# Transposes of six of sixteen FFN blocks move from the matrix engine to 96 SBUF transfers and 12 VectorE transposes

## The chip, the cores and the metric

The kernel runs on one core of a Trainium2 chip. The metric is the device time of one execution in microseconds (us), the lower the better. The engines are named as the profile names them: PE (TensorE, the matrix engine; PEld is its weight loads), DVE (VectorE), ACT (ScalarE), POOL (GpSimd) and SP (SyncE, which here only issues transfers).

## The reference

The input is 4096 rows (two sequences of 2048) of 256 numbers, all float32. A feed-forward part, a linear attention and the feed-forward part again are each added to the rows; each works on rows that were normalized first.

```python
x = x + 0.5 * ffn(layernorm(x), W_r, W_k, W_v, mu_r, mu_k)
x = x + attention(layernorm(x), Wq, Wk, Wv, Wu, Wo)
x = x + 0.5 * ffn(layernorm(x), W_r, W_k, W_v, mu_r, mu_k)
# ffn:
x_prev = concatenate([zeros, x[:, :-1, :]])          # the row before, 0 ahead of a sequence
xr = mu_r * x + (1 - mu_r) * x_prev
xk = mu_k * x + (1 - mu_k) * x_prev
out = sigmoid(xr @ W_r) * (square(relu(xk @ W_k)) @ W_v)
# attention, 16 heads of 16:
q, k = relu(x @ Wq) / 4, relu(x @ Wk) / 4            # v = x @ Wv, u = silu(x @ Wu)
out = (srms_norm(q @ (k.T @ v)) * u) @ Wo
```

## The kernel before

The rows are cut into 8 blocks of 512 (four tiles of 128 rows). "FFN n" is the feed-forward part on block n for n = 0 to 7 (the first one) and on block n - 8 for n = 8 to 15 (the second one). Each product in float32 is made of three in float32r, from operands split in a rounded part (`_hi`) and a rest (`_lo`), so most of the work of ACT, DVE and POOL is splitting.

For the mixing of FFN n the normalized rows `xn` must stand with the features on the partitions, since `mu` goes by features and the row before is then the column before. Before the change eight 128x128 transposes on PE do that (`transpose_a(n)`, L1296), from `xn` into the PSUM tile `psA`. From `psA` ACT takes the previous-row part (`previous`, L635), DVE adds the current-row part (`mix_current`, L948), ACT and POOL split the mix in `mix_k_hi` (`mix_high`, L668) and `mix_k_lo` (`k_low`, L427), and ACT and DVE the other one in `mix_r_hi` and `mix_r_lo` (`r_low`, L976). `xn` is one buffer, and its scales come from `stats_a` (DVE, L917), `scales_a` (POOL, L402 to L411) and `normalize` (ACT, L618).

Each engine has its instructions written out by hand in one order, and a wait on a semaphore holds all that stands behind it on that engine. The part of the program that matters here is a loop over i = 1 to 6 on ACT, DVE and POOL ("iteration i") with the same on PE. In iteration i, PE does `ffn_k(i)` (into `psK`), `transpose_a(i + 1)`, `transpose_b(i - 1)` (rows of the attention, L1410), `ffn_r(i)`, `k_and_u(i - 1)` (keys and gates of the attention), `ffn_v(i)`, `gram(i - 1)` (into `psK`, reads `k_hi` and `k_lo`) and `q_of(i - 1)`. All products show as lines L1279 to L1281. Iterations 5 and 6 and the part behind them hold attention outputs too (`attend`, `transpose_g`, `project_out`; `gate_heads` and `head_norms` on DVE). Behind iteration 6, FFN 7 is done without a next mix, and FFN 8 is mixed apart.

Four waits tie the engines together at the places below. `k_and_u` waits for `x2_low` of DVE (L1024), which waits for `x2_high` of ACT (L712). `gram` waits for both halves of `k_lo` (`kt_low` on POOL, L479), which waits for `kt_high` of ACT (L722). `ffn_k(i + 1)` waits for `keep_g(i - 1)` of DVE (L1048 for a batch's first block, L1051), since both use the first bank of `psK`. And `normalize` waits for the last of the four instructions of `scales_a`. SP only issues: 17 loads at the start, and the stores of the last stage, each behind its wait.

Of the kernel before, what the change touches and what calls it, by code (L numbers as in the profile page):

```python
# [45 lines left out]
def macaron(nc, x, w_t, mu_r, mu_k, out):  # L46
# [6 lines left out]
    with ExitStack() as ctx:  # L53
# [3 lines left out]
        def sem(name):  # L57
            return ctx.enter_context(nc.semaphore(name))
# [233 lines left out]
        def prev_part(n, rk, h):  # L292

            return mix_part(n, rk, h) + n

        def half(g):
            return slice(g * D, (g + 1) * D)

# [47 lines left out]
        def _(sp):  # L346
# [22 lines left out]
            sp.dma_start(wo[:], weight_rows("o")).then_inc(s_w_in["o"], 16)  # L369
            for b in range(3, NB):  # L370
                load_x(b)
            for b in range(NB - 1):
                store_x(b)
            for t in range(TILES):
# [7 lines left out]
        def _(pool):  # L382
# [150 lines left out]
            for i in range(1, 6):  # L533
                act_low(i)
                k_low(i + 1)
                if i > 1:
                    kt_low(i - 1)
                scales_a(i + 2)
                scales_b(i)
                x1_low(i)  # L540
                if i == 1:
                    weight_sum("v")
                if i == 2:
                    pool.wait_ge(s_wo_hi, 1)
                    nc.gpsimd.tensor_tensor(wo_lo[:], wo[:], wo_hi[:].bitcast(F32), ALU.subtract).then_inc(s_wo_lo, 1)
# [48 lines left out]
        def _(act):  # L594
# [202 lines left out]
            for i in range(1, 7):  # L797
                front(i, i + 1, i - 1)
                sigmoid_u(i - 1, 0)
                sigmoid_r(i, 1)  # L800
                sigmoid_u(i - 1, 1)
                if i > 1:
                    kt_high(i - 1, 0)
                sigmoid_u(i - 1, 2)
                sigmoid_u(i - 1, 3)
                if i > 1:
                    kt_high(i - 1, 1)
                if i == 6:
                    keep_g_rows(0)
                mix_high(i + 1, 1)  # L810
                if i <= 5:
                    normalize(i + 2)
                if i >= 5:
                    square_heads(i - 5)
                x1_high(i)
                if i == 2:
                    act.wait_ge(s_w_in["o"], 16)
                    nc.scalar.activation(wo_hi[:], wo[:], ACT.Identity).then_inc(s_wo_hi, 1)
                relu_q(i - 1)
# [70 lines left out]
        def _(dve):  # L890
# [53 lines left out]
            def mix_one(n, rk, h):  # L944

                dve.wait_ge(s_prev, prev_part(n, 1, h))
                m = mix[:, rk, h, :]
                nc.vector.scalar_tensor_tensor(out=m, in0=psA[:, h, :], scalar=mu[:, rk, h:h + 1], in1=m,  # L948
                                               op0=ALU.mult, op1=ALU.add).then_inc(s_mix, 1)

            def mix_first(rk, g, h):

# [226 lines left out]
            for i in range(1, 7):  # L1179
                if 1 < i <= 5:  # L1180
                    stats_a(i + 2)
                x2_low(i - 1)
                mix_current(i + 1)
                if i == 1:
# [29 lines left out]
            add_attention(1)  # L1214
            stats_b(7)
            gate_heads(2)
            head_norms(2)
            x2_low(7)
            keep_g(6)
# [57 lines left out]
        def _(pe):  # L1277
# [283 lines left out]
            q_of(0, (s_silu, 2))  # L1561
            for i in range(2, 5):
                ffn_k(i, [(s_gacc, i - 1)])
                transpose_a(i + 1, [(s_wcen, 4)] if i == 4 else [])
                transpose_b(i - 1)
                ffn_r(i)
                k_and_u(i - 1)
# [5 lines left out]
            kv(0, [(s_halo, 7)])  # L1573

            ffn_k(5, [(s_gacc, 4)])
            transpose_a(6, [(s_kvbd, 1)])
            transpose_b(4)
            ffn_r(5)
            k_and_u(4)
# [3 lines left out]
            q_of(4, (s_silu, 18))  # L1583

            ffn_k(6, [(s_gacc, 5)])
            transpose_a(7, [(s_gu, 2)])
            transpose_b(5)
            ffn_r(6)
            k_and_u(5)
# [14 lines left out]
            attend(2, [(s_gu, 4)])  # L1604
            q_of(6, (s_x2, 4))

            transpose_a(8, [(s_gu, 6)])
            transpose_b(7)
            gram(6)
            k_and_u(7)  # L1610
# [64 lines left out]
```

## Time and profile before

| | |
|---|---|
| time, median of 3 runs | 312.41 us (312.12 to 312.45) |
| the profiled execution | 312.87 us, span of the core 311.1 us |
| PE busy | 303.8 us, 98% of the span |
| DVE / ACT / POOL busy | 240.4 / 235.6 / 214.8 us (77 / 76 / 69%) |
| granted clock of PE | 1.00 from 46 us to the end |
| transfers | 10.85 MB, of which hardly any between 37 us and 230 us |

The profiled execution took 312.87 us, of which 1.8 us lie outside the core's span. Busy shares tell which engine is full, but each matrix product ends later than the next one starts, so for PE the starts of its weight loads are the better clock: a group of eight or of twelve ends where the next group's first weight load starts.

### The profile page before, as it was taken

The page shows a single profiled execution, that of the slowest core. Times are in us where ns is not written, and L with a number is a line of the kernel's source. Part 1 is how long each engine was busy: PE and PEld are TensorE (multiplying, and loading weights), DVE is VectorE, ACT ScalarE, POOL GpSimd, SP SyncE. Part 2 cuts the span into 40 slices and gives each one's busy share as a digit, 9 for nine tenths or more (in the row PEclk, how much of TensorE's full clock was granted, in tenths as well). Part 3 has the DMA queues.
Part 4 walks back from the last instruction along what each step waited for, and adds up shares of the span by engine and source line. Part 5 has one row for each costly group of instructions (what it writes and reads, how often), then busy time and mean ns, then how long its engine had stood idle before and what let it go on. Part 6 is the DMA issues. An engine that isn't in the chain of part 4 may idle for free.

```text
span 311.1 us, 5822 instructions
## 1 busy us (share of the span) xinstructions
PE 303.8 (98%) x2044; PEld 276.8 (89%) x2044; DVE 240.4 (77%) x586; ACT 235.6 (76%) x461; POOL 214.8 (69%) x236
## 2 busy tenths in 40 slices
PE   6899999999999999999999999999999999999995
PEld 6688889889988988988988998989999999999984
DVE  2989893585666746896894699586979797999695
ACT  2886958879589579679349548669797979699981
POOL 4387978779777688669269314815798979769833
PEclk9999999999999999999999999999999999999999
DMA  7960000000000000000000000000001010101023
GB/s 207 382 223 0 1 3 0 0 2 0 2 1 3 0 0 2 0 2 0 0 3 1 2 0 0 2 1 3 0 3 67 2 67 16 54 2 67 32 106 135
DMA packets 10752, 10.85 MB, mean 35 GB/s; under 512 B 482, under 2 KB 10724, under 8 KB 10724
## 3 DMA queue, kind: packets, MB, share of 16 engines
q1 hardware_dynamic: 10432, 10.23, 9.6%
q8 instruction: 16, 0.26, 0.4%
q10 hardware_dynamic: 292, 0.26, 0.2%
q14 instruction: 12, 0.10, 0.1%
HBM read 6.29 MB, written 4.19 MB: 34 GB/s over the span
## 4 chain that ended last, share of the span: by engine, by line
PE 79%; DVE 12%; ACT 4%; issue 2%; POOL 1%; DVEq 0%; ACTq 0%; POOLq 0%
PE psK L1279 7%; PE psK L1281 7%; PE psK L1280 7%; PE psX L1279 7%; PE psX L1281 7%; PE psX L1280 7%; PE psRV L1280 6%; PE psRV L1279 6%; PE psRV L1281 6%; PE psA L1296 3%; DVE mix L948 3%; PE psA L1483 2%; PE psX L1410 2%; PE psX L1496 2%; PE psK L1483 2%
## 5 line engine op out<-in xcount | busy, mean ns | idle before, releaser
L948 DVE SCALAR_TENSOR_TENSOR mix<-psA,mu,mix 128x512 f32<-128x512 f32 x60 | 41.5, 744 | 11.4 <-ACT mix L635 11.4
L618 ACT ACTIVATE xn<-xs,shiftA,rstdA 128x256 f32<-128x256 f32 x53 | 27.7, 607 | 15.9 <-POOL shiftA L411 15.9
L427 POOL TENSOR_TENSOR mix_k_lo<-mix,mix_k_hi 128x512 fp32r<-128x512 f32 x26 | 33.3, 1301 | 8.5 <-ACT mix_k_hi L668 8.5
L635 ACT ACTIVATE mix<-psA,one_mu 128x511 f32<-128x511 f32 x60 | 36.9, 697 | 0.6 <-PE psA L1296 0.6
L1279 PE MATMUL psRV<-ffn_hi,mix_r_hi 128*128 128x256 f32 x120 | 34.3, 286 | 0.0
L1281 PE MATMUL psRV<-ffn_hi,mix_r_lo 128*128 128x256 f32 x120 | 33.6, 280 | 0.0
L1280 PE MATMUL psRV<-ffn_lo,mix_r_hi 128*128 128x256 f32 x120 | 33.5, 280 | 0.0
L1279 PE MATMUL psRV<-ffn_hi,act_hi 128*128 128x256 f32 x96 | 27.5, 286 | 0.0
L1280 PE MATMUL psRV<-ffn_lo,act_hi 128*128 128x256 f32 x96 | 26.8, 279 | 0.0
L1281 PE MATMUL psRV<-ffn_hi,act_lo 128*128 128x256 f32 x96 | 26.8, 279 | 0.0
L479 POOL TENSOR_TENSOR k_lo<-k_tok,k_hi 128x512 fp32r<-128x512 f32 x14 | 18.1, 1295 | 11.4 <-ACT k_hi L722 11.4
L917 DVE BATCH_NORM_STATS2 statsA<-xs 128x6 f32<-128x256 f32 x64 | 22.4, 413 | 2.6 <-DMA xs<-x_dram 2.5
L1279 PE MATMUL psK<-mix_k_hi,ffn_hi 128*128 128x512 f32 x60 | 24.1, 402 | 0.0
L470 POOL TENSOR_TENSOR x_lo<-xs,x_hi 128x512 fp32r<-128x512 f32 x14 | 17.8, 1295 | 8.6 <-ACT x_hi L717 8.6
L1281 PE MATMUL psK<-mix_k_hi,ffn_lo 128*128 128x512 f32 x60 | 23.5, 392 | 0.0
L1280 PE MATMUL psK<-mix_k_lo,ffn_hi 128*128 128x512 f32 x60 | 23.4, 391 | 0.0
L1279 PEld LDWEIGHTS psRV<-ffn_hi,mix_r_hi 128*128 128x128 f32 x120 | 22.5, 188 | 0.4 <-issue 0.2
L1280 PEld LDWEIGHTS psRV<-ffn_lo,mix_r_hi 128*128 128x128 f32 x120 | 22.6, 188 | 0.2
L1281 PEld LDWEIGHTS psRV<-ffn_hi,mix_r_lo 128*128 128x128 f32 x120 | 22.5, 187 | 0.0
L1024 DVE TENSOR_TENSOR x_lo<-psX,x_hi 128x512 fp32r<-128x512 f32 x16 | 10.3, 683 | 14.4 <-ACT x_hi L712 14.4
L668 ACT ACTIVATE mix_k_hi<-mix 128x512 fp32r<-128x512 f32 x30 | 18.8, 658 | 1.9 <-DVE mix L948 1.8
L668 ACT ACTIVATE mix_r_hi<-mix 128x512 fp32r<-128x512 f32 x30 | 17.7, 648 | 0.8 <-DVE mix L948 0.8
(204 smaller groups left out, 1084.5 us busy)
## 6 DMA issues: line engine op xcount, KB each, us to landing
xs<-x_dram SPq DMA_DIRECT2D x7, 512.0 KB, 7.8
out_dram<-xs SPq DMA_DIRECT2D x7, 512.0 KB, 2.9
out_dram<-xs SPq DMA_DIRECT2D x4, 128.0 KB, 1.8
xs<-x_dram ACTq DMA_DIRECT2D x2, 128.0 KB, 3.0
xs<-x_dram SPq DMA_DIRECT2D x2, 128.0 KB, 2.8
silu_u<-w_ffn_k_dram SPq DMA_DIRECT2D x1, 256.0 KB, 5.1
silu_u<-w_ffn_r_dram SPq DMA_DIRECT2D x1, 256.0 KB, 6.2
q_store<-w_k_dram SPq DMA_DIRECT2D x1, 256.0 KB, 6.4
```

The costliest lines, as they stand in the source:

```text
L427: nc.gpsimd.tensor_tensor(mix_k_lo[:, h, :], mix[:, 0, h, :], mix_k_hi[:, h, :].bitcast(F32), ALU.subtract).then_inc(s_lo_k, 1)
L470: nc.gpsimd.tensor_tensor(x1_lo[:, g * BANK:(g + 1) * BANK], row(xs, a, g * BANK, BANK), x1_hi[:, g * BANK:(g + 1) * BANK].bitcast(F32), A ...
L479: nc.gpsimd.tensor_tensor(k_lo[:, tiles, :], k_tok[:, tiles, :], k_hi[:, tiles, :].bitcast(F32), ALU.subtract).then_inc(s_kt_lo, 1)
L618: nc.scalar.activation(xn[:, t, :], tile_row(xs, b, t), ACT.Identity, bias=shiftA[:, t:t + 1], scale=rstdA[:, t:t + 1]).then_inc(s_xn, 1)
L635: nc.scalar.activation(mix[:, rk, h, 1:BLOCK], psA[:, h, 0:BLOCK - 1], ACT.Copy, scale=one_mu[:, rk, h:h + 1]).then_inc(s_prev, 1)
L668: nc.scalar.activation(hi[:, h, :], mix[:, rk, h, :], ACT.Identity).then_inc(done, 1)
L917: nc.vector.bn_stats(statsA[:, t, :], tile_row(xs, b, t)).then_inc(s_bnA, 1)
L948: nc.vector.scalar_tensor_tensor(out=m, in0=psA[:, h, :], scalar=mu[:, rk, h:h + 1], in1=m, op0=ALU.mult, op1=ALU.add).then_inc(s_mix, 1)
L1279: nc.tensor.matmul(dst, a_hi, b_hi, start=start, stop=False)
L1280: nc.tensor.matmul(dst, a_hi, b_lo, start=False, stop=False)
L1281: return nc.tensor.matmul(dst, a_lo, b_hi, start=False, stop=stop)
L1483: last = nc.tensor.matmul(ps[:, t // 2, (t % 2) * D + h * P:(t % 2) * D + (h + 1) * P], q_half(j, h)[:, tok(t)], kv_bd[:, j // BB, h, :], ...
```

## The change

For FFN 3 to 8 (`TURNED`) PE no longer transposes. Instead SP waits until all four tiles of `xn` are written and issues 16 transfers of 32 partitions x 8 x 32 numbers (32 KB each) inside SBUF. They put block column j of `xn` on partition group j of a spare buffer (`squares` for FFN 3 to 5, `wsum` for FFN 6 to 8), in pieces of 32 numbers (128 bytes). DVE waits for all 16 (`s_quads`) and turns the 32x32 blocks with two instructions (`turn`), one for each half of the features, straight into `psA`. Beside that, ACT's `normalize(i + 2)` now stands ahead of `mix_high(i + 1, 1)`, and POOL's `scales_a(i + 2)` ahead of `kt_low(i - 1)`. The spare buffers are not new.

```diff
@@ sync
+            for n in TURNED:
+                sp.wait_ge(*normalized(n, TILES - 1))
+                for j in range(QUADS):
+                    for i in range(QUADS):
+                        rows = quads_of(n)[j * QUAD:(j + 1) * QUAD, i * D:(i + 1) * D]
+                        sp.dma_start(rows.rearrange("c (th f) -> c th f", f=QUAD),
+                                     xn[i * QUAD:(i + 1) * QUAD, :, :].rearrange(
+                                         "c t (h j f) -> c (t h) j f", h=HALVES, j=QUADS)[:, :, j, :]
+                                     ).then_inc(s_quads, 16)
             for b in range(NB - 1):
                 store_x(b)
@@ gpsimd
                 k_low(i + 1)
+                scales_a(i + 2)
                 if i > 1:
                     kt_low(i - 1)
-                scales_a(i + 2)
                 scales_b(i)
@@ scalar
-                mix_high(i + 1, 1)
                 if i <= 5:
                     normalize(i + 2)
+                mix_high(i + 1, 1)
@@ vector
+            def turn(n, free=()):
+                for s, v in free:
+                    dve.wait_ge(s, v)
+                dve.wait_ge(s_halo, n + 1)
+                dve.wait_ge(s_quads, 16 * QUADS * QUADS * (n - TURNED[0] + 1))
+                rows = quads_of(n).rearrange("p (i t h f) -> p h t i f", i=QUADS, t=TILES, h=HALVES)
+                for h in range(HALVES):
+                    nc.vector.transpose(psA[:, h, :].rearrange("p (t i c) -> p t i c", t=TILES, i=QUADS),
+                                        rows[:, h, :, :, :]).then_inc(s_tA, 1)
...
                     stats_a(i + 2)
+                if i + 1 in TURNED:
+                    turn(i + 1, {5: [(s_wcen, 4)], 6: [(s_kvbd, 1)], 7: [(s_gu, 2)]}.get(i + 1, ()))
                 x2_low(i - 1)
                 mix_current(i + 1)
...
             gate_heads(2)
+            turn(8, [(s_gu, 6)])
             head_norms(2)
             x2_low(7)
@@ tensor
-                transpose_a(i + 1, [(s_wcen, 4)] if i == 4 else [])
...
-            transpose_a(6, [(s_kvbd, 1)])
...
-            transpose_a(7, [(s_gu, 2)])
...
-            transpose_a(8, [(s_gu, 6)])
```

On DVE, this is the place between iterations 1 and 2, before the change (`L976` is `r_low(2)`, `L1048` `keep_g(0)`, `L917` and `L928` `stats_a(4)`, `L1024` `x2_low(1)`):

```order
L976 TENSOR_TENSOR mix_r_lo<-mix,mix_r_hi 128x512 x2
L1048 COPY g_acc<-psK 128x512
L917 BN_STATS statsA<-xs 128x6 x4
L928 BN_AGGR meanvarA<-statsA 128x2 x4
L1024 TENSOR_TENSOR x_lo<-psX,x_hi 128x512 x2
L948 SCALAR_TENSOR_TENSOR mix<-psA,mu,mix 128x512 x4
L961 TENSOR_TENSOR halo<-one_mu,psA 128x4
```

And this is the same place of the change, whose lines stand 20 to 30 further down in the file:

```order
L1006 TENSOR_TENSOR mix_r_lo<-mix,mix_r_hi 128x512 x2
L1078 COPY g_acc<-psK 128x512
L937 BN_STATS statsA<-xs 128x6 x4
L948 BN_AGGR meanvarA<-statsA 128x2 x4
L978 STREAM_TRANSPOSE psA<-squares 128x512 x2
L1054 TENSOR_TENSOR x_lo<-psX,x_hi 128x512 x2
L968 SCALAR_TENSOR_TENSOR mix<-psA,mu,mix 128x512 x4
```

The two transposes and their wait stand ahead of `x2_low(1)`, on which PE's `k_and_u(1)` waits.

On POOL, this is iteration 2 before the change (`L427` is `k_low(3)`, `L479` `kt_low(1)`, `L402` to `L411` `scales_a(4)`):

```order
L427 TENSOR_TENSOR mix_k_lo<-mix,mix_k_hi 128x512 x2
L479 TENSOR_TENSOR k_lo<-k_tok,k_hi 128x512 x2
L402 TENSOR_SCALAR var_epsA<-meanvarA 128x4
L407 TENSOR_TENSOR rstdA<-var_epsA,minus_half 128x4
L409 TENSOR_TENSOR mean_rstdA<-meanvarA,rstdA 128x4
L411 TENSOR_SCALAR shiftA<-mean_rstdA 128x4
```

And this is the same place of the change:

```order
L447 TENSOR_TENSOR mix_k_lo<-mix,mix_k_hi 128x512 x2
L422 TENSOR_SCALAR var_epsA<-meanvarA 128x4
L427 TENSOR_TENSOR rstdA<-var_epsA,minus_half 128x4
L429 TENSOR_TENSOR mean_rstdA<-meanvarA,rstdA 128x4
L431 TENSOR_SCALAR shiftA<-mean_rstdA 128x4
L499 TENSOR_TENSOR k_lo<-k_tok,k_hi 128x512 x2
```

The four small instructions now stand ahead of `kt_low(1)`, on which PE's `gram(1)` waits.

On ACT, this is the end of iteration 1 before the change (`L668` is `mix_high(2, 1)`, `L618` `normalize(3)`, `L717` `x1_high(1)`, `L744` `relu_q(0)`):

```order
L738 ACTIVATE silu_u<-psK,rstdB 128x256
L668 ACTIVATE mix_r_hi<-mix 128x512 x2
L618 ACTIVATE xn<-xs,shiftA,rstdA 128x256 x4
L717 ACTIVATE x_hi<-xs 128x1024
L744 ACTIVATE q_store<-psX 128x512 x2
```

And this is the same place of the change:

```order
L758 ACTIVATE silu_u<-psK,rstdB 128x256
L638 ACTIVATE xn<-xs,shiftA,rstdA 128x256 x4
L688 ACTIVATE mix_r_hi<-mix 128x512 x2
L737 ACTIVATE x_hi<-xs 128x1024
L764 ACTIVATE q_store<-psX 128x512 x2
```

`normalize(3)` and its wait for `scales_a(3)` now stand ahead of `mix_high(2, 1)`, on which DVE's `r_low(2)` waits. On PE nothing changes but the six groups of eight transposes that are gone, and on SP 96 issues stand between the loads and the first store.

## Rows read from the trace of the kernel before

**Rows 1.** The page: busy time, share of the span, instructions.

```profile
PE 303.8 (98%) x2044; PEld 276.8 (89%) x2044; DVE 240.4 (77%) x586; ACT 235.6 (76%) x461; POOL 214.8 (69%) x236
```

**Rows 2.** The chain in order of time: start us, us, piece.

```profile
48.95 0.87 PE psA L1296 x8
```

**Rows 3.** Timeline of DVE, iterations 1 to 3: start us, us, instruction, count, [idle before, releaser].

```profile
43.20 1.26 DVE L976 TENSOR_TENSOR mix_r_lo<-mix,mix_r_hi 128x512 fp32r<-128x512 f32 x2
44.38 0.69 DVE L1048 COPY g_acc<-psK 128x512 f32<-128x512 f32 x1
...
50.93 1.29 DVE L1024 TENSOR_TENSOR x_lo<-psX,x_hi 128x512 fp32r<-128x512 f32 x2 [4.28 <-ACT x_hi L712]
...
66.49 0.68 DVE L1051 TENSOR_TENSOR g_acc<-g_acc,psK 128x512 f32<-128x512 f32 x1
...
72.23 1.29 DVE L1024 TENSOR_TENSOR x_lo<-psX,x_hi 128x512 fp32r<-128x512 f32 x2 [3.46 <-ACT x_hi L712]
```

**Rows 4.** Timeline of ACT, iterations 1 to 3.

```profile
38.17 1.21 ACT L668 ACTIVATE mix_r_hi<-mix 128x512 fp32r<-128x512 f32 x2
42.07 2.08 ACT L618 ACTIVATE xn<-xs,shiftA,rstdA 128x256 f32<-128x256 f32 x4 [2.69 <-POOL shiftA L411]
...
59.07 0.48 ACT L731 ACTIVATE k_tok<-psK,rstd2B 128x256 f32<-128x256 f32 x1 [0.47 <-PE psK L1281]
...
59.80 0.63 ACT L722 ACTIVATE k_hi<-k_tok 128x512 fp32r<-128x512 f32 x1
...
71.59 1.09 ACT L712 ACTIVATE x_hi<-psX 128x512 fp32r<-128x512 f32 x2
```

**Rows 5.** Timeline of POOL, iteration 2.

```profile
54.88 2.55 POOL L427 TENSOR_TENSOR mix_k_lo<-mix,mix_k_hi 128x512 fp32r<-128x512 f32 x2 [0.97 <-ACT mix_k_hi L668]
...
60.51 1.30 POOL L479 TENSOR_TENSOR k_lo<-k_tok,k_hi 128x512 fp32r<-128x512 f32 x1 [1.26 <-ACT k_hi L722]
61.89 0.52 POOL L402 TENSOR_SCALAR var_epsA<-meanvarA 128x4 f32<-128x4 f32 x1
...
63.97 0.20 POOL L411 TENSOR_SCALAR shiftA<-mean_rstdA 128x4 f32<-128x4 f32 x1
```

**Rows 6.** Timeline of PEld: first weight loads of four products, iterations 2 and 3.

```profile
45.84 0.19 PEld L1279 LDWEIGHTS psK<-mix_k_hi,ffn_hi 128*128 128x128 f32 x1
...
53.25 0.19 PEld L1279 LDWEIGHTS psX<-att_hi,x_hi 128*128 128x128 f32 x1
...
61.58 0.19 PEld L1279 LDWEIGHTS psK<-k_hi,x_hi 128*128 128x128 f32 x1
...
67.22 0.19 PEld L1279 LDWEIGHTS psK<-mix_k_hi,ffn_hi 128*128 128x128 f32 x1 [0.21 <-DVE g_acc L1051]
```

**Rows 7.** DMA: the main queue, then issues by line with KB and us to landing.

```profile
q1 hardware_dynamic: 10432, 10.23, 9.6%
...
out_dram<-xs SPq DMA_DIRECT2D x7, 512.0 KB, 2.9
out_dram<-xs SPq DMA_DIRECT2D x4, 128.0 KB, 1.8
```

**Rows 8.** Issues by source line: duration ns min/median/max, first and last start.

```profile
L348 SPq DMA_DIRECT2D xs<-x_dram x7: 469/1157/1277, 2.2 to 13.2; - x7
L354 SPq DMA_DIRECT2D out_dram<-xs x7: 372/373/388, 233.4 to 304.5; - x7
```

**Rows 9.** Timelines of DVE and PEld around `k_and_u(5)`.

```profile
139.35 1.29 DVE L1024 TENSOR_TENSOR x_lo<-psX,x_hi 128x512 fp32r<-128x512 f32 x2 [0.26 <-ACT x_hi L712]
...
141.67 0.19 PEld L1279 LDWEIGHTS psX<-att_hi,x_hi 128*128 128x128 f32 x1
```

**Rows 10.** Timelines of DVE and PEld ahead of `k_and_u(7)`.

```profile
175.22 0.69 DVE L1038 TENSOR_TENSOR g_lo<-psX,g_hi 128x512 fp32r<-128x512 f32 x1 [0.52 <-ACT g_hi L760]
...
187.46 1.28 DVE L1024 TENSOR_TENSOR x_lo<-psX,x_hi 128x512 fp32r<-128x512 f32 x2
...
188.86 0.19 PEld L1279 LDWEIGHTS psX<-att_hi,x_hi 128*128 128x128 f32 x1
```

More of the change, by code:

```diff
@@ L168, in macaron @@
         s_tA = sem("s_tA")
+        s_quads = sem("s_quads")
         s_prev = sem("s_prev")
@@ L294, in prev_part, with quads_of @@
             return mix_part(n, rk, h) + n
+        TURNED = range(3, 9)
+        QUAD = 32
+        QUADS = P // QUAD
+        def quads_of(n):
+            return (squares[:].rearrange("p g e -> p (g e)") if n < 6
+                    else wsum[:].rearrange("p n e -> p (n e)"))
         def half(g):
```

## The prediction, made before the changed kernel ran

> **What bounds the kernel now.** I read the page first: PE is busy for 98% of the span, the other engines for 69 to 77% [rows 1]. So time that PE loses is lost to the end, and time that PE saves is won only as far as nothing else is as late as PE. Next the chain in order of time: the eight transposes of one FFN block stand in it as one piece of 0.87 us [rows 2]. Then the timelines of the engines, one stage at a time, for the distance between what PE needs and when it is there. Three distances are short. Ahead of `ffn_k(3)` PE already waited 0.21 us for DVE's `keep_g` [rows 6], which ended at 67.17 [rows 3]. `x2_low(1)` ended at 52.22 [rows 3], only 1.0 us ahead of its user `k_and_u(1)` at 53.25 [rows 6]. And `x2_low(7)` ended at 188.74, 0.1 us ahead of `k_and_u(7)` at 188.86, behind a stretch in which DVE was never idle since 175.22 [rows 10].
>
> **What is removed.** Six pieces of 0.87 us on PE [rows 2]: 5.2 us if nothing else became late.
>
> **What is added: the transfers.** Let D be the time from the end of `normalize(n)` to the landing of the last of the 16 transfers. An issue by SP took 0.37 us for 512 rows of a store, and 0.47 to 1.28 us in the loads at the start, where transfers queued up [rows 8]. A store of 128 KB landed 1.8 us after its issue, one of 512 KB 2.9 us [rows 7]: 1.1 us for 24 rows of 1 KB more on each of 16 engines, 46 ns for a row, and so about 1.4 us without rows. A row of the new transfers is 128 bytes, and each of 16 engines gets 16 of them and a semaphore write. No row shows such a piece. Below, it costs an eighth of 46 ns: 0.1 us for a transfer, the issues decide, and D is 15 x 0.37 + 1.6 = 7.2 us. Above, it costs the full 46 ns: 17 x 46 ns = 0.78 us for a transfer, the DMA engines decide, and D is 16 x 0.78 + 1.4 = 13.9 us. I take issues of 0.40 us and a last landing of 1.8 us, D = 7.8 us, since a piece up to 24 ns leaves the issues in the lead and the bytes are few.
>
> **What is added: DVE.** Two instructions of 128x512. The trace has no transpose on DVE. The nearest row is the copy `g_acc<-psK` of the same shape, 0.69 us [rows 3]. The lower bound is half of it, the upper one twice. I take 0.69 us each, 1.38 us for a block. For this a page speaks against the change: the Trainium skill, "VectorE: DVE Perf Modes", sections "The three transpose paths" and "Rules for kernel authors", leaves a 128x128 transpose that may end in PSUM to TensorE and gives VectorE's 32x32 grid of one 128x128 tile (bf16) as 311 ns. By that figure eight tiles would be an estimate of 2.5 us a block, 1.1 us more than by the row at each of the three places below where DVE decides, and the sum would be 3.3 us more. No run here shows it yet, so the sum goes by the row.
>
> **Step by step.**
> 1. *`mix_high(2, 1)` behind `normalize(3)`.* `shiftA` of FFN 3 does not come sooner (POOL's order is the same in iteration 1), so `normalize(3)` still runs from 42.07 to 44.15, and `mix_r_hi(2)`, before at 38.17 to 39.4, runs to 45.35 [rows 4]. `r_low(2)`, before at 43.20, then ends at 46.05, and the `keep_g(0)` queued behind it (0.69) at 46.75 [rows 3]. `ffn_k(2)`, before at 45.84 [rows 6], waits for it: +0.9.
> 2. *`turn(3)` ahead of `x2_low(1)`.* 44.15 + 7.8 + 1.38 + 1.29 = 54.6 is the end of `x2_low(1)`. PE is there without a wait at 53.25 + 0.9 - 0.87 = 53.3. So `k_and_u(1)` starts at 54.6 where it was 53.25 [rows 6]: +1.35, step 1 and the saving of this block included.
> 3. *`kt_low` behind `scales_a`, iteration 2.* The four instructions take 64.17 - 61.89 = 2.3 us with their gaps [rows 5]. `k_low(3)`, before from 54.88, starts 1.9 us later, since the mix on DVE follows `x2_low`; it ends at 59.35, `scales_a` at 61.6, the halves of `k_lo` (1.30 each) at 62.9 and 64.2. `gram(1)` starts at 61.58 + 1.35 = 62.9 [rows 6] and reads the second half 0.7 us later, at 63.6: +0.6. The wait of 0.21 at `ffn_k(3)` is covered by that, so the sum there is 1.35 + 0.6 - 0.2 = +1.75.
> 4. *Iteration 3.* `x2_high` of ACT at 71.59 + 1.75 [rows 4] is later than the end of `turn(4)`, so the transfers are hidden. But of the 0.87 us only 0.47 come through: ACT had no more idle time than that ahead of the last `k_tok` [rows 4], and ACT, then DVE's chain to `keep_g`, decide when `ffn_k(4)` may start, as they did for `ffn_k(3)` with its wait for `g_acc` at 67.22 [rows 6]. -0.45.
> 5. *Iterations 4 and 5.* PE saves 0.87 us each and comes to `gram` that much sooner, while POOL comes with `k_lo` 2.3 us later than before on the first half. By the offsets of iteration 2 without its delay: `k_low` ends at 57.43 [rows 5], `scales_a` at 59.7, `k_lo` at 61.0 and 62.3; `gram` would start at 60.7 and read the second half 0.7 us later. 0.3 + 0.6 = 0.9 us of wait: the sum is 0.
> 6. *Iteration 6.* `normalize(7)` is 12 us ahead of its use, so D is hidden. DVE is full: it is free at 139.09 and `x2_low(5)` followed at 139.35, after 0.26 us of idle time [rows 9]. Its chain starts 0.45 us sooner (step 4's reason) and gets 1.38 us more: `x2_low(5)` ends at 139.09 - 0.45 + 1.38 + 1.29 = 141.3. `k_and_u(5)`, before at 141.67 [rows 9], could start at 140.8. 0.5 us of wait, -0.4.
> 7. *`turn(8)` ahead of `head_norms(2)` and `x2_low(7)`.* `x2_low(7)` ends at 188.74 + 1.38 = 190.1; PE is there at 188.86 - 0.87 = 188.0 [rows 10]: 2.1 us of wait, +1.25.
>
> The sum is 1.75 - 0.45 + 0 - 0.4 + 1.25 = +2.15 us: waits of 7.35 us against 5.2 us saved. From the profiled execution's 312.87 us that makes 315.0; the profiled one is 0.46 us above the median of 312.41, so in the medians 314.6 us.
>
> **The rivals.**
> - *The small pieces bind the DMA engines.* For it: half of a piece's possible price, 6 to 46 ns, lies above 24 ns. Against it: the queue's 10.2 MB took 9.6% of 16 engines [rows 7], and 128-byte pieces may cost little more than their bytes. Then D counts twice: in step 2, and in the loop from one `x2_low` over `k_and_u`, `kt_high` and `normalize` (7.2 us from the start at 53.25 to the end of `k_hi` at 60.43, 2.08 us of `normalize` [rows 4, 6]: 9.3 us) and D and 2.67 us of DVE back to the next. Before, that loop took 72.23 - 50.93 = 21.3 us [rows 3], so it decides from D = 9.3 us on. At 30 ns a piece D is 9.6 us and the time some 317 us. At 46 ns D is 13.9, step 2 gives 6.1 us more, three loops 4 us more each, FFN 7 some 3 us: 337 us. The Trainium skill, "DMA: Bandwidth & Descriptors", section "Why small descriptors are slow (HBM only)", says that transfers from SBUF to SBUF are spared the penalty of small packets. By that D would be at its lower end, 7.2 us, and the sum 0.6 us less.
> - *`x2_low` is not held: faster.* The turns would have to end ahead of `x2_high` at all three places where I let DVE decide. That takes 1.25, 0.5 and 2.1 us out of the sum: -1.7, 310.7 us. It decides from the point where these three waits together are below 1.7 us instead of 3.85. For it: DVE was idle for 4.28 us ahead of `x2_low(1)` [rows 3]. Against it: that needs D below 51.83 - 44.15 - 1.38 = 6.3 us, less than 15 issues and a landing, and at the other two places there was 0.26 us of idle time or none [rows 9, 10].
> - *`gram` does not wait for `k_lo`: the same.* If POOL and ACT come to `k_lo` sooner than by steps 3 and 5, those give 0.6 and 1.3 us back: +0.25, 312.7 us. For it: PE's distances to `k_lo` are a few tenths, and a `var_epsA` of 0.52 us for 128x4 numbers [rows 5] could well be shorter at another moment. Against it: before, the second half of `k_lo` ended at 61.81 [rows 5] and `gram` read it at 62.3, so there was 0.5 us of room, and 2.3 us of work moves ahead of it, of which only 1.26 us was idle time.
>
> **How the numbers follow.** The sum 0.52 (its own range 313.3 to 316.2, from D between 7.2 and 8.7 and half a us for the waits of `gram`); DMA-bound 0.20; not held 0.18; no wait for `k_lo` 0.10. 0.2% is 0.6 us, about what this measurement can tell from no change. So faster 0.18, same 0.10, slower 0.72. The range of eight in ten goes from 311.5 us, which leaves out most of the faster case, to 320.0 us, which leaves out the upper half of the DMA-bound one.
>
> **What would show it.** Right: SP's 16 issues of a block take 6 to 7 us, and `turn(3)` ends near 53.3; `ffn_k(2)` starts near 46.75; PE waits for DVE's `x_lo` ahead of `k_and_u(1)`, (5) and (7) and for POOL's `k_lo` ahead of `gram`; the transposes take 0.69 us. Wrong: a block's issues take over 8 us, or DVE waits for the transfers in iterations 3 to 5 (the first rival); PE has no wait of 1 us or more ahead of `k_and_u(7)` (the second); the transposes take twice the copy, which adds 1.4 us at each of the three places.

## The result

The changed kernel took 338.18 us in the median of 4 runs (335.87 to 339.89), the kernel before 312.43 us on the same chip: a ratio of 1.0818 (95% interval 1.0791 to 1.0845), 8% slower. The prediction was 314.6 us with a range from 311.5 to 320.0 us: the direction is right, the size wrong by a factor of twelve. The profiled execution took 339.89 us, of which 338.1 us are the core's span. Where runs of a kernel lay more than 1.5% above its fastest one, its time and ratio below are those of the others; this touches the rows of 1 KB alone.

The page of the changed kernel, beside [rows 1]:

```profile
span 338.1 us, 5834 instructions
PE 311.4 (92%) x1996; PEld 280.4 (83%) x1996; DVE 247.0 (73%) x598; ACT 237.2 (70%) x461; POOL 213.1 (63%) x236
PEclk9799999699599699789999999999999999999999
q1 hardware_dynamic: 36544, 13.38, 14.5%
PE 55%; SPq 14%; DVE 12%; ACT 6%; POOL 5%; issue 4%; DMA 3%; DVEq 0%; ACTq 0%; POOLq 0%
```

PE's share fell from 98% to 92%, though its busy time rose by 7.6 us with 48 transposes fewer: work done at a lower clock. The clock row gives each slice of 8.5 us in tenths, and it falls four times in the stretch of iterations 2 to 5. The queue of the transfers is busy for 14.5% of 16 engines over the span, and in a stretch in which they run (48 to 54 us, in the windows below) the share is 0.30, so the DMA engines are no bound. But the fourth part of the page has an owner that it did not have before: SPq, the issuing of transfers by SP, holds 14% of the chain that ended last.

The transfers of the change, by the line that issues them: duration of an issue in ns (min/median/max), first and last start, then who waited, and the time from an issue to its landing, beside [rows 7, 8]:

```profile
L388 SPq DMA_DIRECT2D squares<-xn x48: 585/611/1663, 44.9 to 109.2; - x48
L388 SPq DMA_DIRECT2D wsum<-xn x48: 585/611/1421, 125.6 to 204.6; - x48
...
  DVE psA L978: 26.1, 5
...
DMA to landing us min/median/max: 1.9/1.9/3.0
```

An issue takes 0.61 us where a store took 0.37. In the chain of FFN 3 the issues start at 44.89, 45.68, 46.32, 46.98 and so on, 0.65 us apart. The first issue of FFN 4 to 8, with the queue long empty, takes 0.58 to 0.59 us as well, so the price is not that of a queue filling up. DVE waited 26.1 us for them, in five blocks.

The timeline of DVE in iteration 2, beside [rows 3]:

```profile
48.55 0.36 DVE L948 BATCH_NORM_AGGREGATE meanvarA<-statsA 128x2 f32<-128x6 f32 x4
56.83 1.32 DVE L978 STREAM_TRANSPOSE psA<-squares 128x512 f32<-128x512 f32 x2 [7.92 <-DMA squares<-xn]
58.06 1.26 DVE L1054 TENSOR_TENSOR x_lo<-psX,x_hi 128x512 fp32r<-128x512 f32 x2
```

`turn(3)` starts at 56.83, 7.9 us after DVE came to it. `normalize(3)` ended at 44.87 (from 42.79, 2.08 long). So D, from there to the start of `turn(3)`, is 12.0 us (the last landing, at 56.73, is 0.1 us sooner). For FFN 4 to 6 it is 12.8, 12.9 and 13.3 us: the second issue of each took 1.4 to 1.7 us (the maxima above) in place of 0.6. Beside each of the three the trace has a load of 16 KB on the queue of instructions. Other issues beside such loads were not held, so that these are the cause is likely and not shown. The two transposes take 1.32 us together with their overlap.

The first weight loads of four products of PE, beside [rows 6, 9, 10] ("issue" here is PE waiting; the table of waits puts 18.9 us in 6 waits ahead of `k_and_u` down to DVE's `x_lo`):

```profile
47.37 0.19 PEld L1312 LDWEIGHTS psK<-mix_k_hi,ffn_hi 128*128 128x128 f32 x1 [0.76 <-DVE g_acc L1078]
...
59.43 0.28 PEld L1312 LDWEIGHTS psX<-att_hi,x_hi 128*128 128x128 f32 x1 [5.53 <-issue]
...
86.52 0.29 PEld L1312 LDWEIGHTS psX<-att_hi,x_hi 128*128 128x128 f32 x1 [4.02 <-issue]
...
215.94 0.19 PEld L1312 LDWEIGHTS psX<-att_hi,x_hi 128*128 128x128 f32 x1 [1.82 <-issue]
```

And PE alone in windows of this kernel: window, its length, PE busy (instructions), granted clock, DMA share, GB/s:

```profile
48.00:54.00 6.00, 6.00 (x43) 1.00 0.30 49
54.00:59.40 5.40, 0.11 (x1) 0.89 0.15 24
59.40:65.20 5.80, 5.74 (x14) 0.52 0.00 0
65.20:80.00 14.80, 14.80 (x95) 1.00 0.15 24
86.50:92.20 5.70, 5.65 (x13) 0.50 0.00 0
```

The clock fell while PE stood idle ahead of `k_and_u(1)`, and its first 12 to 14 products ran at the lower of the two levels (1.2 of 2.4 GHz). They follow each other 0.43 us apart, against 0.23 us at the full clock. That is some 2.6 us more for `k_and_u`, and nothing in the prediction stood for it.

The starts of `k_and_u(a)` show where the time went. They are read from the same kind of row in each kernel; the last five lines are experiments that follow.

| kernel | a = 1 | 1 to 2 | 2 to 3 | 3 to 4 | 4 to 5 | 5 to 6 | 6 to 7 |
|---|---|---|---|---|---|---|---|
| before | 53.25 | 21.3 | 21.9 | 22.2 | 23.0 | 25.9 | 21.3 |
| changed | 59.43 | 27.1 | 27.3 | 27.7 | 26.1 | 25.8 | 22.6 |
| 4 wide transfers | 53.09 | 21.2 | 21.2 | 22.1 | 23.4 | 25.8 | 22.6 |
| 16 to DRAM | 55.26 | 22.4 | 21.5 | 22.0 | 23.3 | 25.8 | 22.7 |
| 12 transfers | 57.06 | 23.5 | 22.6 | 22.3 | 22.7 | 25.8 | 22.7 |
| filled waits | 59.45 | 23.8 | 23.9 | 25.5 | 24.9 | 27.2 | 22.6 |
| fastest | 53.19 | 20.4 | 21.1 | 21.5 | 22.7 | 25.8 | 21.3 |

The changed kernel is 6.2 us late at the first one (0.8 of it from the start of the program, ahead of all this), loses 5.8, 5.4, 5.5 and 3.1 us in the four loops behind it, gains 0.1 in the next, and loses 1.3 us in the last. Together that is 27.1 us, and the spans differ by 27.0.

### The profile page after: what moved, and what is told of

The parts are those of the page before. It is cut to its first block, busy times and chain, and to the rows that moved or that the text cites. A ratio compares the mean times of both kernels' runs of the same rounds, so it can differ in the third digit from the quotient of the medians.

```text
span 338.1 us, 5834 instructions
## 1 busy us (share of the span) xinstructions
PE 311.4 (92%) x1996; PEld 280.4 (83%) x1996; DVE 247.0 (73%) x598; ACT 237.2 (70%) x461; POOL 213.1 (63%) x236
## 3 DMA queue, kind: packets, MB, share of 16 engines
q1 hardware_dynamic: 36544, 13.38, 14.5%
## 4 chain that ended last, share of the span: by engine, by line
PE 55%; SPq 14%; DVE 12%; ACT 6%; POOL 5%; issue 4%; DMA 3%; DVEq 0%; ACTq 0%; POOLq 0%
SPq L388 14%; PE psX L1312 7%; PE psX L1314 6%; PE psX L1313 6%; PE psK L1312 5%; PE psK L1314 4%; PE psK L1313 4%; PE psRV L1312 4%; PE psRV L1314 4%; PE psRV L1313 4%; ACT xn L638 3%; DVE psA L978 2%; DVE x_lo L1054 2%; PE psX L1529 2%; DMA squares<-xn 2%
## 5 line engine op out<-in xcount | busy, mean ns | idle before, releaser
L655 ACT ACTIVATE mix<-psA,one_mu 128x511 f32<-128x511 f32 x60 | 36.8, 691 | 14.5 <-DVE psA L978 14.5
L447 POOL TENSOR_TENSOR mix_k_lo<-mix,mix_k_hi 128x512 fp32r<-128x512 f32 x26 | 33.1, 1294 | 22.0 <-ACT mix_k_hi L688 21.9
L1312 PE MATMUL psX<-att_hi,x_hi 128*128 128x512 f32 x32 | 17.0, 533 | 18.9 <-DVE x_lo L1054 18.9
L638 ACT ACTIVATE xn<-xs,shiftA,rstdA 128x256 f32<-128x256 f32 x53 | 27.7, 608 | 6.0 <-POOL shiftA L431 6.0
L1312 PEld LDWEIGHTS psX<-att_hi,x_hi 128*128 128x128 f32 x32 | 8.1, 253 | 21.6 <-issue 19.9
L1314 PE MATMUL psK<-mix_k_hi,ffn_lo 128*128 128x512 f32 x60 | 23.5, 392 | 0.0
L1313 PE MATMUL psK<-mix_k_lo,ffn_hi 128*128 128x512 f32 x60 | 23.4, 390 | 0.0
L1313 PEld LDWEIGHTS psRV<-ffn_lo,mix_r_hi 128*128 128x128 f32 x120 | 22.6, 188 | 0.2
```

The costliest lines, as they stand in the source:

```text
L447: nc.gpsimd.tensor_tensor(mix_k_lo[:, h, :], mix[:, 0, h, :], mix_k_hi[:, h, :].bitcast(F32), ALU.subtract).then_inc(s_lo_k, 1)
L638: nc.scalar.activation(xn[:, t, :], tile_row(xs, b, t), ACT.Identity, bias=shiftA[:, t:t + 1], scale=rstdA[:, t:t + 1]).then_inc(s_xn, 1)
L655: nc.scalar.activation(mix[:, rk, h, 1:BLOCK], psA[:, h, 0:BLOCK - 1], ACT.Copy, scale=one_mu[:, rk, h:h + 1]).then_inc(s_prev, 1)
L1312: nc.tensor.matmul(dst, a_hi, b_hi, start=start, stop=False)
L1313: nc.tensor.matmul(dst, a_hi, b_lo, start=False, stop=False)
L1314: return nc.tensor.matmul(dst, a_lo, b_hi, start=False, stop=stop)
```

## The experiments

All are compared with runs of the kernel before on the same chip (312.4 to 312.5 us).

**The order on ACT and POOL alone, transposes on PE.** To see what the reordering costs without the transfers.

```diff
@@ gpsimd (before.py)
                 k_low(i + 1)
+                scales_a(i + 2)
                 if i > 1:
                     kt_low(i - 1)
-                scales_a(i + 2)
@@ scalar: normalize(i + 2) ahead of mix_high(i + 1, 1)
```

> The kernel before with only two of the change's edits: scales_a ahead of kt_low on POOL, normalize ahead of mix_high(i + 1, 1) on ACT. The transposes stay on PE. Theory (the loss lies in the time D to the landing of the last transfer, set by SP's issues): by steps 1 and 3 of the prediction, without the savings, ffn_k(2) waits some 0.9 us and gram some tenths in iterations 2, 4 and 5, so 313.3 to 315.5 us and a clock of 1.00 throughout. Rival (the new order on ACT and POOL makes most of the 26 us): 320 us or more.

314.28 us (313.50 to 314.54), ratio 1.0052 (1.0034 to 1.0070), granted clock 0.995 to 1.00. It costs 1.8 us, a small part of the 26. `ffn_k(2)` waits for `keep_g(0)` as step 1 said:

```profile
46.02 0.19 PEld L1279 LDWEIGHTS psK<-mix_k_hi,ffn_hi 128*128 128x128 f32 x1 [0.81 <-DVE g_acc L1048]
```

**No transfers.** D is taken away, all other edits stay.

```diff
-            for n in TURNED: ... (the 16 transfers)
@@ turn
-                dve.wait_ge(s_quads, ...)
-                rows = quads_of(n).rearrange(...)
+                dve.wait_ge(*normalized(n, TILES - 1))
+                rows = xn[:].rearrange(...)
```

> The changed kernel without its 96 transfers: turn waits for normalize and transposes xn where it stands, so the blocks stay in their partition group and FFN 3 to 8 get wrong columns. Two DVE instructions a block, as in the change. Theory: D is 0 here, turn ends ahead of x2_high in iterations 1 to 5, PE waits a little at k_and_u(5) and some 2 us at k_and_u(7): 311.0 to 315.0 us, and the granted clock stays at 1.00. Rival (DVE's transposes, the order on ACT and POOL, or FFN 7 and 8 cost most of it): 320 us or more.

313.11 us, ratio 1.0019 (1.0008 to 1.0030), clock 1.00. So 25 of the 26 us hang on the transfers. Even with D at nothing there is no gain: 5.2 us are off PE, and waits take them back. The table of PE's waits in this kernel (us in total, times, longest):

```profile
PE psK L1302 <- POOL k_lo L489: 2.0, 4, 0.6
PE psX L1302 <- DVE x_lo L1044: 1.6, 1, 1.6
...
PE psK L1302 <- DVE g_acc L1068: 0.4, 1, 0.4
```

By the starts of the weight loads these waits are 2.8, 1.8 and 0.8 us.

**Four wide transfers: pieces or issues?** The same bytes in the same pieces of 128 bytes, but a quarter of the issues.

```diff
-                    for i in range(QUADS):
-                        rows = quads_of(n)[j * QUAD:(j + 1) * QUAD, i * D:(i + 1) * D]
-                        sp.dma_start(rows..., xn[i * QUAD:(i + 1) * QUAD, :, :]...[:, :, j, :])
+                    sp.dma_start(quads_of(n)[:, j * D:(j + 1) * D]..., xn[:]...[:, :, j, :])
```

> The changed kernel with 4 transfers of 128 partitions a block in place of 16 of 32: the same bytes in the same pieces of 128 bytes, but each row stays on its partition, so FFN 3 to 8 get wrong columns. If SP's issues decide (0.65 us each): 4 issues and a landing, D about 4.6 us, below the 6.3 us from which x2_low is held in iteration 1, so 311 to 315 us. If the pieces or their bytes decide (the first rival of the prediction): D stays near 12 us and the time between 330 and 340 us. If an issue's duration grows with its number of pieces, each of the 4 takes some 2 us, D is 9 to 10 us and the time 316 to 325 us.

313.29 us, ratio 1.0016 (1.0005 to 1.0026). D fell to 4.7 us and the loss is gone, with as many small pieces as in the change. Its issues, and their landing:

```profile
L386 SPq DMA_DIRECT2D squares<-xn x12: 594/692/1574, 44.1 to 86.1; - x12
...
  DVE psA L975: 0.7, 1
...
DMA to landing us min/median/max: 2.4/2.7/3.7
```

An issue with 1024 pieces takes 0.69 us, one with 256 takes 0.61. So an issue hardly grows with its pieces. The landing does: 1.9 us with 16 pieces for each of 16 engines, 2.7 us with 64 in the median and 2.4 us in the blocks without a long issue (FFN 3, 7 and 8), which is an estimate of 11 to 17 ns for a piece. That is below the 24 ns up to which the prediction let the issues lead. The Trainium skill, "DMA: Bandwidth & Descriptors", section "Rules for kernel authors", says of many small transfers that they should be made one large one; by that rule, the trace agrees (4.7 us in place of 12.0).

**Rows of 1 KB.** The same 16 issues, with 32 pieces each in place of 256.

```diff
-                        sp.dma_start(rows.rearrange("c (th f) -> c th f", f=QUAD), xn[...][:, :, j, :])
+                        sp.dma_start(quads_of(n)[j * QUAD:(j + 1) * QUAD, i * D:(i + 1) * D],
+                                     xn[i * QUAD:(i + 1) * QUAD, j, :])
```

> The changed kernel with 16 transfers a block as in the change, of the same 32 KB between the same partition groups, but each of 32 rows of 1 KB in place of 256 pieces of 128 bytes; the numbers stand in another arrangement, so FFN 3 to 8 get wrong columns. If the 0.65 us of an issue come from its 256 pieces, an issue takes 0.37 to 0.45 us as a store of rows of 1 KB does, D is 7.5 to 8.5 us and the time 313.5 to 317 us. If 0.65 us is the price of any issue of this kind, D stays near 12 us and the time near 338 us.

327.5 us (all runs 326.04 to 333.64, the profiled one the slowest), ratio 1.048 (1.042 to 1.054). The issues:

```profile
L387 SPq DMA_DIRECT2D squares<-xn x48: 507/591/1495, 44.8 to 106.5; - x48
```

0.59 us with 32 pieces, 0.61 with 256: the price of an issue is not that of its pieces. D is 11.5 us, near the second expectation, but the time lies between the two, some 11 us below the changed kernel's. The profiled execution shows a part of why: for FFN 4 to 6 D is 12.3 to 12.5 us where the changed kernel has 12.8 to 13.3, and the granted clock in the 5.5 to 5.7 us behind the second to fourth wait is 0.70 to 0.73 where that kernel has 0.50 to 0.52. The rest is open.

**Twelve transfers.** Between 4 and 16.

```diff
-                    for i in range(QUADS): ...
+                    for p0, p1 in ((0, 32), (32, 64), (64, P)):
+                        sp.dma_start(quads_of(n)[p0:p1, j * D:(j + 1) * D]..., xn[p0:p1]...[:, :, j, :])
```

> The changed kernel with 12 transfers a block in place of 16, whose rows stay on their partitions (FFN 3 to 8 get wrong columns); pieces of 128 bytes. D is 11 x 0.65 + 2.3, about 9.4 us. Theory (D is hidden in the loop up to 9.3 us and counts once for each block beyond it): x2_low(1) held by 3.1 us, the loops by next to nothing, so 315.5 to 319 us. Rival (every issue between 4 and 16 costs the same, because something is late in proportion to them): 313.3 + 8 x 2.07 = 330 us.

318.56 us (317.55 to 320.37), ratio 1.0182 (1.0154 to 1.0209). D is 9.7 us. `x2_low(1)` is held, and `k_and_u(1)` waits 3.27 us (3.1 expected). The first two loops are 2.3 and 1.4 us longer than those of the four wide transfers, where next to nothing was expected: D of FFN 4 is 10.1 us, and the clock is down there too (0.72 between 57 and 63 us). The loss isn't proportional to the issues: the step from 4 to 12 costs 5.3 us, the one from 12 to 16 another 19.6.

**Over DRAM: the changed kernel with the D that was predicted.** One store of `xn` and four loads.

```diff
+                sp.dma_start(scratch, xn[:]...).then_inc(s_scratch, 16)
+                sp.wait_ge(s_scratch, 16 * (n - TURNED[0] + 1))
+                for j in range(QUADS):
+                    sp.dma_start(quads_of(n)[j * QUAD:(j + 1) * QUAD, :]...,
+                                 scratch.rearrange("(i c) (j e) -> c j i e", ...)[:, j, :, :])
...
@@ scalar: normalize writes xn with its columns in another order
```

> The changed kernel with the same result, but the blocks of xn go to a scratch buffer in DRAM in one transfer of 512 KB and come back in four of 128 KB (normalize writes xn in another order of its columns, so that the pieces are 1 KB): five issues in two stages in place of 16. By the rows of the changed kernel and of the four wide transfers, D is 0.4 + 2.9 + 3 x 0.65 + 2.5, about 7.5 us, close to the 7.8 us of the prediction. Theory (only D was mis-sized): step 2 as predicted, x2_low(1) held by 1.3 us, iterations 2 to 5 unheld, 313.8 to 315.5 us at a clock of 1.00. Rival (something else of the transfers costs the 26 us): 320 us or more.

313.25 us (312.82 to 314.09), ratio 1.0028 (1.0016 to 1.0040). It is a little below the expectation, since D is 6.9 us and not 7.5; `k_and_u(1)` waits 0.43 us. For FFN 4 D is 8.6 us, which the loop still hides. Its transfers on SP's timeline (FFN 3), then the loads by line:

```profile
43.77 0.34 SPq L387 DMA_DIRECT2D scratch<-xn  x1
46.37 1.76 SPq L391 DMA_DIRECT2D squares<-scratch  x4
```

```profile
L391 SPq DMA_DIRECT2D squares<-scratch x12: 302/432/434, 46.4 to 87.7; - x12
```

Two trips in a row, 1 MB in place of 0.5, and it is 5 us sooner than 16 transfers inside SBUF. An issue takes 0.34 us from SBUF to DRAM and 0.43 us from DRAM to SBUF.

**Sixteen to DRAM: is it the kind of transfer?** The transfers of 32 rows of 1 KB again, but they end in DRAM.

```diff
-                        sp.dma_start(quads_of(n)[j * QUAD:(j + 1) * QUAD, i * D:(i + 1) * D],
+                        sp.dma_start(scratch[i * QUAD:(i + 1) * QUAD, j * D:(j + 1) * D],
                                      xn[i * QUAD:(i + 1) * QUAD, j, :])
...
@@ vector: turn reads xn; @@ scalar: normalize writes xn with its columns in another order
```

> The changed kernel with 16 transfers a block of 32 partitions x 1 KB as in the variant with rows of 1 KB, but to a scratch buffer in DRAM instead of SBUF; turn waits for them and transposes xn where it stands, so FFN 3 to 8 get wrong columns. If the price of an issue hangs on both ends being in SBUF: 0.34 to 0.40 us an issue, D of 7.2 to 8 us, the D that the prediction took, and 313 to 315 us. If it hangs on the 32 partitions or on the number of issues in a row: 0.6 us, D of 11.4 us, 326 to 334 us.

316.81 us (315.43 to 317.28), ratio 1.0140 (1.0116 to 1.0165), between the two expectations and nearer to the first. The issues:

```profile
L389 SPq DMA_DIRECT2D scratch<-xn x96: 302/421/1474, 44.1 to 178.6; - x96
```

0.42 us against 0.59 with the other end in SBUF. So the kind of transfer makes most of the difference to a store's 0.37 us. Those of FFN 3 start 0.46 us apart, from 44.12 to 51.01, and the last lands 1.6 us after its issue. D is 8.6 us, 0.8 more than the prediction took for the change, and the time 2.2 us above it.

**Filled waits: what does the clock cost?** Products that nobody uses, in the waits ahead of `k_and_u(1)` to `k_and_u(4)`.

```diff
+            def warm_up(i):
+                pe.wait_ge(s_relu, 2 * (i + 1))
+                for _ in range({2: 20, 3: 14, 4: 12, 5: 13}[i]):
+                    nc.tensor.matmul(psK[:, 1, :], ffn_hi[:, 0, 0, 0:P], ffn_hi[:, 0, :, :]..., start=True, stop=True)
...
                 ffn_r(i)
+                warm_up(i)
                 k_and_u(i - 1)
... (the same ahead of k_and_u(4))
```

> The changed kernel with 20, 14, 12 and 13 unused products of 128x512 on PE in the waits ahead of k_and_u(1) to k_and_u(4), written where k_and_u writes over them. Nothing else is changed, D stays 12 us. Theory (the fall of the granted clock behind each wait adds some 2.7 us to k_and_u, which stands in the loop, so the loop is 27.2 where D alone gives 24): the clock stays near 1.00, the loop becomes 24 to 25 us and the time 323 to 330 us. Rival (the clock costs nothing because PE waits anyway): 336 to 340 us; if the products delay k_and_u, more.

328.63 us (328.29 to 331.09), ratio 1.0532 (1.0493 to 1.0571): 9.5 us faster than the changed kernel by doing more work. PE in windows of this kernel, where the changed one had 0.89 and 0.52:

```profile
54.00:59.40 5.40, 4.65 (x21) 1.00 0.15 24
59.40:63.50 4.10, 4.02 (x18) 1.00 0.00 0
```

`k_and_u(1)` starts at 59.45 as in the changed kernel, but the next one follows after 23.8 us, not 27.1. `normalize(4)` starts 2.6 us sooner (66.50, where the changed kernel has 69.07):

```profile
69.07 2.07 ACT L638 ACTIVATE xn<-xs,shiftA,rstdA 128x256 f32<-128x256 f32 x4
```

So the slow products stand in the loop, and the clock costs it on top of D. From the start of `k_and_u` to the end of `normalize` it is 9.1 to 9.2 us in each of the four loops, against 11.6 to 11.8 in the changed kernel: 2.6 us a loop. The rest of the 3.3 us in the first loop is the long issue of FFN 4, which is missing here (D is 11.8 us, not 12.8). In later blocks it is the other way round (13.8 and 13.2 us for FFN 6 and 7, against 13.3 and 11.8), and in sum the four D are equal. In this execution the clock still fell behind a wait of 2.75 us at `k_and_u(5)` (0.72 between 157 and 163 us), which is why its next loop is 27.2 us.

**The fastest: D hidden, nothing else late.** Over DRAM for FFN 4 to 7 alone; FFN 3 and 8 stay on PE. POOL's four small instructions go where POOL has time, ahead of `k_low(i + 1)`.

```diff
+        TURNED = range(4, 8)
... (the route over DRAM as above; transpose_a(3) and transpose_a(8) back on PE)
@@ gpsimd
+                if i > 1:
+                    scales_a(i + 2)
                 k_low(i + 1)
                 if i > 1:
                     kt_low(i - 1)
@@ scalar: normalize(i + 2) ahead of mix_high(i + 1, 1) for i = 2 to 5 only
```

> The route over DRAM for FFN 4 to 7 alone, FFN 3 and 8 transposed on PE as before; scales_a(i + 2) stands ahead of k_low(i + 1) on POOL for i = 2 to 5, so that it holds neither kt_low nor normalize, and ACT and POOL keep the order of before in iteration 1. Same result as the reference. Theory: normalize ends some 2 us sooner than in the changed kernel, D of 7.5 us is hidden, gram doesn't wait for k_lo; of 4 x 0.87 us saved some 0.5 us are lost at k_and_u(5): 309.0 to 310.5 us. Rival (ACT and DVE, not PE, then set the pace in iterations 2 to 6): 311 to 313 us.

309.96 us (309.90 to 310.20), ratio 0.9919 (0.9904 to 0.9934): 2.6 us faster than the kernel before. What PE still waits for in iterations 3 to 6, by its weight loads, beside 0.22 us ahead of `ffn_k(3)`, which were there before (0.21, [rows 6]):

```profile
83.43 0.19 PEld L1323 LDWEIGHTS psK<-k_hi,x_hi 128*128 128x128 f32 x1 [0.39 <-POOL k_lo L501]
...
108.88 0.97 PEld L1505 LDWEIGHTS psA<-wv,g_acc 128*128 128x128 f32 x8 [0.46 <-issue]
...
138.97 0.19 PEld L1323 LDWEIGHTS psX<-att_hi,x_hi 128*128 128x128 f32 x1 [0.61 <-issue]
```

**Its order alone, transposes on PE.**

```diff
@@ before.py, gpsimd and scalar: the two moves above, nothing else
```

> The kernel before, transposes on PE, with the two order edits of the fastest variant alone: scales_a(i + 2) ahead of k_low(i + 1) on POOL and normalize(i + 2) ahead of mix_high(i + 1, 1) on ACT, for i = 2 to 5. Theory (that variant wins by the 4 x 0.87 us off PE, and its order only keeps waits away): 312.0 to 313.5 us. Rival (its order is what wins): 309.5 to 311 us.

312.42 us, ratio 1.0000 (0.9988 to 1.0013). As expected, the order wins nothing by itself; it keeps waits out of the way of the 4 x 0.87 us off PE.

**Its order with the 16 transfers of the change.**

```diff
@@ fastest, sync: the 16 transfers of the change in place of the store and the four loads
```

> The fastest variant (FFN 4 to 7, its order on ACT and POOL) with the 16 transfers of the change in place of the route over DRAM. Same result as the reference. Theory: D is 12 us again. normalize(4) ends near 64.3, turn(4) near 77.7 where x2_high is there at 72: held by 4.5 us, then two loops of 24 us against some 20.6 of PE, each with up to 2.7 us for the clock behind it: 318 to 327 us. Rival (the better order alone would have saved the change): 309.5 to 312 us.

323.43 us (322.00 to 324.16), ratio 1.0345 (1.0315 to 1.0374), within the expectation. `k_and_u(2)` to `k_and_u(5)` wait 3.75, 2.97, 2.13 and 1.74 us. No order of ACT and POOL that was tried makes up for 12 us.

**The fastest with FFN 8 on DVE too.** Step 7 by itself.

```diff
-        TURNED = range(4, 8)
+        TURNED = range(4, 9)
@@ vector
             gate_heads(2)
+            turn(8, [(s_gu, 6)])
             head_norms(2)
             x2_low(7)
@@ tensor
-            transpose_a(8, [(s_gu, 6)])
```

> The fastest variant with FFN 8 turned on DVE as well, where the change has it: turn(8) ahead of head_norms(2) and x2_low(7), transfers over DRAM. It isolates step 7 of the prediction (+1.25 us; D is hidden here). By the wait of 1.8 us ahead of k_and_u(7) in the changed kernel, less the 0.87 us off PE: +0.9 to +1.3 us, 310.8 to 311.3 us. Rival (DVE has room there): 309.1 us.

311.36 us (310.86 to 311.99), ratio 0.9970 (0.9960 to 0.9981): 1.4 us slower than without, a little more than expected. `k_and_u(7)` follows `k_and_u(6)` after 22.6 us where it was 21.3. DVE has no room there.

D against time, in one table. D is the distance from the end of `normalize(3)` to the start of `turn(3)`, in the profiled execution. Without transfers nothing has to land, and `turn(3)` starts after 4.0 us because DVE comes to it then:

| kernel | issues a block | D, us | time, us |
|---|---|---|---|
| no transfers | 0 | none | 313.1 |
| 4 wide | 4 | 4.7 | 313.3 |
| over DRAM | 1 + 4 | 6.9 | 313.3 |
| 16 to DRAM | 16 | 8.6 | 316.8 |
| 12 | 12 | 9.7 | 318.6 |
| 16, rows of 1 KB | 16 | 11.5 | 327.5 |
| changed | 16 | 12.0 | 338.2 |

## Why the prediction was wrong

**The step that failed: the size of D.** "I take issues of 0.40 us and a last landing of 1.8 us, D = 7.8 us." The landing measured 1.9 us, the issues 0.65 us apart, and D 12.0 us. The price was taken from the stores [rows 8]. They go from SBUF to DRAM, while the new transfers stay in SBUF, and the trace before had no issue with SBUF at both ends. In the experiments the one kind runs at 0.34 to 0.42 us at the same place of the program, the other at 0.59 to 0.69. I put the upper bound of D (13.9 us) on the pieces and left none for the issue, so that the case in which D is 12 us had a chance of 0.20 and a cause that is not the real one. The sign that was named for being wrong did come: a block's issues took 10.55 us, not 6 to 7, and DVE waited for them in iterations 2 to 6.

**The first rival, half right.** "The small pieces bind the DMA engines" is refuted by the four wide transfers, which have the same pieces and lose nothing. But what it said of a long D is what happened: D counts once in step 2 and again in each loop from one `x2_low` to the next. Its arithmetic of the loop holds at the full clock: 9.3 us from the start of `k_and_u` to the end of `normalize`, and 9.1 us in the kernel with filled waits (59.45 to 68.57). With D = 12.0 and 2.67 us of DVE that makes a loop of 24.0 us, and that kernel had 23.8 and 23.9. That its 337 us lie next to the 338.2 measured is luck: they were for a D of 13.9 us at the full clock, and the real D is shorter while the clock, which no term stood for, adds some 10 us. (Its own terms, 314.6 + 6.1 + 3 x 4 + 3, make 335.7.)

**The term that was missing: the clock.** In the changed kernel the same stretch takes 11.7 us (59.43 to 71.14), because `k_and_u` runs at the lower level behind the wait. D of that block was 12.8 us (from 71.14 to `turn(4)` at 83.91), and 11.7 + 12.8 + 2.67 is 27.2 us, the loop that was measured. So "it decides from D = 9.3 us on" was too high as well: with 16 transfers to DRAM D is 8.6 us for FFN 3 and 9.1 for FFN 4, the granted clock is 0.88 between 46 and 60 us, `k_and_u` and `normalize` take 10.7 us (55.26 to 65.93), and the first loop is 22.4 us in place of 21.2. For the whole kernel the filled waits give 9.5 us of the 25.7 back. The rest is mostly D itself: 5.4 us at `k_and_u(1)`, and loops of 23.8 to 25.5 us against 21.3 to 23.0 before. The last 1.3 us are those of step 7.

**Step 2, right but for D.** The forecast was +1.35 us at `k_and_u(1)` with D = 7.8. With D = 12.0 the same sum gives 1.35 + 4.2 = 5.5, and 6.2 - 0.8 = 5.4 us was measured (0.8 us is the late start of the profiled execution).

**Step 1, right.** +0.9 was forecast for `ffn_k(2)`. With the order alone and with four wide transfers it waits 0.81 us.

**Steps 3 to 6, right in sum, in part by luck, and only where D is hidden.** From `k_and_u(1)` to `k_and_u(6)` the four wide transfers take 0.5 us less than before; the steps gave 0.4 - 0.45 + 0 - 0.4 = -0.45. The waits for `k_lo` are there (0.82, 0.37, 0.80 and 0.80 us), and so is one of 0.3 us at `k_and_u(5)`. Single loops are off by up to 0.8 us either way (the one to `k_and_u(5)` is 0.4 us longer, where 0.4 less was forecast), and these misses cancel: that the sum agrees within 0.1 us is luck. In the changed kernel itself `gram` never waits for `k_lo`, because PE is later than POOL.

**Step 7, right.** +1.25 was forecast; `k_and_u(7)` comes 1.3 us later behind `k_and_u(6)` in every kernel that has `turn(8)` ahead of it, with a wait of 1.8 us (2.1 forecast). Put back alone it costs 1.4 us.

**DVE's transposes, right.** 0.71 us was the median, 0.69 was taken:

```profile
L978 DVE STREAM_TRANSPOSE psA<-squares x6: 683/706/727, 56.8 to 111.8; 128x512 f32<-128x512 f32 x6
```

The Trainium skill, "VectorE: DVE Perf Modes", section "The three transpose paths", gives 311 ns for a tile of 128x128 bf16 and SBUF as where it goes. No run here has bf16; in float32, four tiles to an instruction and into PSUM, a tile took 0.18 us, so the estimate of 2.5 us a block was too high (1.4 us). What that page advises in "Rules for kernel authors", TensorE for a 128x128 transpose that may end in PSUM, holds for the change, but not because of DVE's time: the blocks must first be carried between partitions. Where that time is hidden it doesn't hold: the fastest kernel turns four blocks on DVE and wins 2.5 us against the same order with PE's transposes (309.96 and 312.42 us).

**The second rival, tested.** "Not held" was to give 310.7 us. With D hidden at iterations 1 to 5 the time is 313.1 to 313.3 us, because steps 3, 6 and 7 stay: its condition was met at the first of the three places alone. The third rival (no wait for `k_lo`) did not happen there: the four waits are in the kernel without transfers and in that with four wide ones.

## What to carry to other kernels

Count the issues of a change before its bytes: 16 of 0.65 us in a row are 10 us in which the data is not there, and four issues of the same bytes took 2.9. Take an issue's price from one of the same kind (which memory at either end), and where the trace has none, give the issue a range of its own. And where a wait ahead of matrix products grows by some microseconds, add what the products behind it cost at the lower clock, above all inside a loop that feeds itself. A delay that is hidden in a loop costs nothing until it is as long as the loop's slack, and then counts at every turn: here next to nothing up to 6.9 us, some 4 us at 8.6, and 25 us at 12.0. Advice for or against an engine hangs on what else the way there costs: the same DVE transposes stand in a kernel that is 26 us slower and in one that is 2.5 us faster.

## What the runs showed of the hardware

- An issue of a transfer by SP, median: from SBUF to DRAM 0.34 us (128 partitions x 4 KB) and 0.42 us (32 x 1 KB), from DRAM to SBUF 0.43 us (32 partitions x 4 KB), from SBUF to SBUF 0.59 us (32 x 1 KB), 0.61 us (32 partitions, 256 pieces of 128 bytes) and 0.69 us (128 partitions, 1024 pieces). The first issue on an empty queue costs as much (0.58 us in the changed kernel). Why SBUF at both ends costs more is open.
- A way over DRAM and back (one store of 512 KB, a wait, four loads of 128 KB) brought all blocks to other partitions in 6.9 us for FFN 3 and 8.6 us for FFN 4, where 16 transfers inside SBUF took 12.0 and 12.8.
- Behind PE's waits of 5.5, 4.0, 3.5 and 3.6 us the granted clock was at its lower level (0.50 to 0.52) for 5.7 us; behind those of 1.4 and 1.8 us at `k_and_u(5)` and `k_and_u(7)` the products ran at the full one. 59 unused products in the waits gave back 9.5 us. The Trainium skill, "TensorE: Matmul & The Clock Gate", section "What's actually happening", has the clock of an idle PE fall to half; the trace agrees.
- ACT wrote `xn` with its columns in another order (pieces of 128 bytes) at no cost: `normalize` took 2.07 us for four tiles either way.
